# Moving each cycle's products with V behind the first scores two cycles later, in a grouped attention kernel with post-layernorm

## The chip, the cores and the metric

The kernel runs on one core of a Trainium2 chip. The metric is the time of one execution on the device in microseconds (us); lower is better. Weights and inputs are in HBM at the start and the result is in HBM at the end.

## The reference

The layer takes x of 1024 rows by 512 columns in float32. What matters here is the attention:

```python
q = jnp.dot(x, Wq).reshape(b, t, H, HD).transpose(0, 2, 1, 3)        # 32 heads of 16
kv = jnp.dot(x, Wkv).reshape(b, t, G, 2, HD).transpose(2, 3, 0, 1, 4)  # 8 groups, 4 heads each
scores = jnp.einsum('bhqd,bhkd->bhqk', q, k)
scores = jnp.where(causal[None, None], -jnp.inf, scores)
weights = jax.nn.softmax(scores * (1.0 / HD ** 0.5), axis=-1)
ctx = jnp.einsum('bhqk,bhkd->bhqd', weights, v)
```

It is followed by the product with Wo and a bias, a residual and a layernorm, then a feed-forward step (one product with W plus eight low-rank updates), a second residual and a second layernorm.

## The kernel before

**Units and cycles.** The attention is cut into 16 units: a unit `u` is one group of four heads with one half of the queries (512 of them). A unit is worked off in cycles; a cycle is one strip `s` of 256 queries against one pair `p` of key blocks of 128. Units 0 to 7 have 3 cycles each, units 8 to 15 have 7 (8 and up see twice the keys): 80 cycles, numbered 0 to 79. In the profiled execution cycle 0 begins at about 36 us, cycle 24 (the first of unit 8) at 126 us and cycle 79 ends at 302 us.

**What a cycle does.** TensorE computes the scores of a cycle in four pieces (three in a cycle on the diagonal), each one matmul of 512 columns into a PSUM bank of its own (`piece_scores`, L1359). ScalarE takes the exponential of each piece into the SBUF buffer `PB` (L853), GpSimd zeroes the part above the diagonal (L693), and TensorE multiplies the result with V (`accumulate`, L1337), on 32 output columns at a time, into bank 6, which holds both strips of a unit. When a strip is done, ScalarE copies it to SBUF (`evacuate`, L767): after cycles 26, 30, 33, 37, 40 and so on in the second half. The score pieces have three banks that go round, so piece number e waits until the exponential of piece e-3 is done. For unit 15, from cycle 71 on, there are six banks.

**The maxima.** Softmax needs the largest score of each row ahead of the exponentials. TensorE computes scores with the query rows on the partitions ("chunks", L1132, 128 to 512 columns each), VectorE reduces each chunk to its maxima (L907, L914), at the end of a unit L928 joins them, GpSimd splits them into three bfloat16 parts (last step L659, semaphore `nm_parts`), TensorE turns them with four small matmuls (`turn_maxima`, L1141) and ScalarE copies the turned rows (L740), from where a DMA takes them into the queries' tile. The turn for unit u stands at the end of a cycle two or three cycles ahead of the unit (`ROWS_AT`): in the second half at the end of cycles 28, 35, 42, 49, 56, 63 and 70.

**The order.** Each engine's order is written out by hand, cycle by cycle. In a cycle TensorE goes through four places j = 0 to 3. At each it issues a lot of that cycle's chunks (`chunks_of_cycle`, spread by `level`; lot 0 is empty in cycles with three chunks), then score piece j, then a part of a filler. Fillers (`FILL`) are the other work: projections, the transposes and products of finished query blocks. Long fillers (the projections Q, the products `WO` and `FF`, all L1195) have a part at each of the four places, short ones (transposes L1255, L1263, and L1242) at places 1 and 3. ScalarE does in a cycle: the copy of a finished strip, then the exponentials, with a normalisation (`first_norm`, `second_norm`, L785) behind the first of them two cycles after a `WO` or `FF` filler, then copies that belong to fillers and the turned rows. `second_norm` falls into cycles 39, 53 and 67.

**Waits around the products.** The product of a cycle waits for its exponentials and masks; the first one of a strip waits for the copy of the strip before (`raw_out`); ScalarE, with three buffers `PB`, waits ahead of cycle c for the product of cycle c-3 (`pv_done`).

Of the kernel before, what the change touches and what calls it, by code (L numbers as in the profile page):

```python
# [19 lines left out]
def postln_kernel(nc, x, wq, wkv, wo, bo, lora_a, lora_b, w, bias, lora_w, xt, out):  # L20
# [26 lines left out]
    NCYC = len(CYCLES)  # L47
# [19 lines left out]
    def pieces(cyc):  # L67

        first = [(0, range(0, 2), 0), (0, range(2, 4), 0)]
        return first + ([(1, range(0, 4), P)] if on_diagonal(cyc) else [(1, heads, 0) for _, heads, _ in first])  # L70

    def last_of(u, s):
        return CYCLES.index((u, s, 2 * half_of(u) + s))

    LAST_OF = {last_of(u, s): (u, s) for u in range(NU) for s in range(2)}
# [29 lines left out]
    def rows_cycle(u):  # L105

        return (FIRST[u] - (LEAD if u > 3 else 2)) if u else -1
# [39 lines left out]
    for n, job in enumerate(STEPS):  # L147
        b, k = divmod(n, 6)
# [137 lines left out]
    with ctx:  # L286
# [122 lines left out]
        def score_bank(e):  # L409

            return MAX_BANKS + e % ST_BANKS if e < WIDE else (e - WIDE) % (MAX_BANKS + ST_BANKS)
# [296 lines left out]
        def _(act):  # L708
# [22 lines left out]
            def middle_part(n):  # L731

                act.wait_ge(*freed(PROJ[n]))
                nc.scalar.activation(parts[:, n % 2, 1, :], rest[:, n % 2, :], ACT.Copy).then_inc(rest_split, 1)

            def turn_rows(u):
                act.wait_ge(nm_turned, rows_turned(u))
                if u >= 3:
                    act.wait_ge(nm_in, 16 * NPART * (u - 2))
                nc.scalar.activation(NMR[0:NPART * REP, u % 2, :], PS[0:NPART * REP, MISC_BANK["rows", u, 0], :],  # L740
                                     ACT.Copy)\
                    .then_inc(nm_rows, 1)
# [17 lines left out]
            def evacuate(u, s):  # L760
                act.wait_ge(pv_done, last_of(u, s) + 1)
                if u >= G:
                    act.wait_ge(we_split, NC)
                if u >= G + 4:
                    act.wait_ge(wo_split, NC)
                cols = slice(s * HQ, (s + 1) * HQ)
                nc.scalar.activation(RAW[:, u, cols], PS[:, PV_BANK, cols], ACT.Copy).then_inc(raw_out, 1)  # L767
# [19 lines left out]
            def first_norm(b):  # L787
                if b >= 2:
                    act.wait_ge(x1b_ready, b - 1)
                    act.wait_ge(t3_done, b - 1)  # L790
                scaled(X1[b % 2], NORM["WO", b], x1_ready)

            def second_norm(b):
                if b >= 2:
                    act.wait_ge(out_done[b % 2], 16 * (b // 2))
                scaled(OUT[b % 2], NORM["FF", b], out_ready)
# [48 lines left out]
            for cyc in range(NCYC):  # L845
                if cyc >= NP_BUF:
                    act.wait_ge(pv_done, cyc - NP_BUF + 1)
                if cyc - 2 in LAST_OF:
                    evacuate(*LAST_OF[cyc - 2])
                for k in range(len(pieces(cyc))):  # L850
                    e = SCORE_BANKS[cyc] + k
                    act.wait_ge(scores, e + 1)
                    nc.scalar.activation(PB[:, cyc % NP_BUF, k, :], PS[:, score_bank(e), :], ACT.Exp, scale=SCALE)\  # L853
                        .then_inc(probs, 1)
                    if k == 0 and cyc == rows_cycle(1) + 1:
                        turn_rows(1)
                    kind, b, _ = FILL.get(cyc - 2, ("", 0, 0))
                    if k == 0 and kind == "WO":
                        first_norm(b)
                    if k == (0 if cyc < NCYC - 1 else len(pieces(cyc)) - 1) and kind == "FF":  # L860
                        second_norm(b)
                kind, b, _ = job = FILL.get(cyc, ("", 0, 0))
                if job in PROJ or kind in BY_ACT:
                    act_job(JOB[job])
                if FILL.get(cyc - 2, ("",))[0] == "WE":
                    act_job(JOB[FILL[cyc - 2]])
                if FILL.get(cyc - 1) in PROJ:
                    middle_part(PROJ.index(FILL[cyc - 1]))
                if kind == "T2":
                    context_high(b, MISC_BANK[job])  # L870
                if kind == "T3":
                    x1_high(b, MISC_BANK[job])
                if cyc in ROWS_AT and ROWS_AT[cyc] > 1:
                    turn_rows(ROWS_AT[cyc])
                if cyc in WO_HIGH_AT:
                    wo_high_half(WO_HIGH_AT.index(cyc))
# [229 lines left out]
        def _(pe):  # L1106
# [30 lines left out]
            def turn_maxima(u):  # L1137
                was_read(MISC_BEHIND["rows", u, 0])
                pe.wait_ge(nm_parts, u + 1)
                for qb in range(TB):  # L1140
                    last = nc.tensor.matmul(PS[0:NPART * REP, MISC_BANK["rows", u, 0], qb * P:(qb + 1) * P],  # L1141
                                            NMP[:, u % 2, qb, :, :].rearrange("p a j -> p (a j)"),
                                            ident_bf[:, :], start=True, stop=True)
                last.then_inc(nm_turned, 1)
# [179 lines left out]
            def accumulate(cyc):  # L1324

                u, s, p = CYCLES[cyc]
                if on_diagonal(cyc):
                    pe.wait_ge(masked, 3 * sum(1 for c in LAST_OF if c <= cyc))
                pe.wait_ge(probs, SCORE_BANKS[cyc + 1])
                if cyc == 0:  # L1330
                    pe.wait_ge(*freed(FIRST_BEHIND[PV_BANK]))
                if p == 0 and u + s:
                    pe.wait_ge(raw_out, 2 * u + s)
                for k, (i, heads, skip) in enumerate(pieces(cyc)):
                    width = HQ - skip
                    for n, j in enumerate(heads):
                        last = nc.tensor.matmul(PS[32 * j:32 * j + 32, PV_BANK, s * HQ + skip:(s + 1) * HQ],  # L1337
                                                VX[:, key_blocks(cyc)[i], u % G, :],
                                                PB[:, cyc % NP_BUF, k, n * width:(n + 1) * width],
                                                start=(p == 0 and i == 0), stop=(on_diagonal(cyc) and i == 1))  # L1340
                last.then_inc(pv_done, 1)

            def piece_scores(cyc, k):

                u, s, _ = CYCLES[cyc]
                i, heads, skip = pieces(cyc)[k]
                kb = key_blocks(cyc)[i]
                e = SCORE_BANKS[cyc] + k
                if e < ST_BANKS:
                    pe.wait_ge(*freed(FIRST_BEHIND[score_bank(e)]))  # L1350
                elif WIDE <= e < WIDE + MAX_BANKS:
                    pe.wait_ge(max_read, len(CHUNKS))
                elif e >= WIDE + MAX_BANKS + ST_BANKS:
                    pe.wait_ge(probs, e - MAX_BANKS - ST_BANKS + 1)
                elif e >= WIDE:
                    pe.wait_ge(probs, WIDE)
                elif e >= ST_BANKS:
                    pe.wait_ge(probs, e - ST_BANKS + 1)
                nc.tensor.matmul(PS[:, score_bank(e), :], KS[0:NROW, u % G, kb * P:(kb + 1) * P],  # L1359
                                 QS[0:NROW, u % SLOTS, heads[0]:heads[-1] + 1, s * HQ + skip:(s + 1) * HQ],  # L1360
                                 start=True, stop=True).then_inc(scores, 1)

            for cyc, (u, _, _) in enumerate(CYCLES):
                if cyc == 0:
                    rows_moved()
                elif cyc == FIRST[u]:
                    pe.wait_ge(nm_in, 16 * NPART * u)
                for j, lot in enumerate(chunks_of_cycle(cyc)):
                    for n in lot:
                        chunk_scores(n)  # L1370
                    if j < len(pieces(cyc)):
                        piece_scores(cyc, j)
                    if cyc == rows_cycle(1) + 1 and j == 0:
                        turn_maxima(1)
                    filler(cyc, j)
                if cyc:
                    accumulate(cyc - 1)
                if cyc in ROWS_AT and ROWS_AT[cyc] > 1:
                    turn_maxima(ROWS_AT[cyc])
            pe.wait_ge(max_read, len(CHUNKS))  # L1380
            pe.wait_ge(probs, SCORE_BANKS[NCYC - 1])
            pe.wait_ge(*freed(MISC_ORDER[-1]))
# [60 lines left out]
```

## Time and profile before

| | |
|---|---|
| time before, median of 3 runs | 341.67 us (341.11 to 341.87) |
| the profiled execution | 340.83 us, its span 339.1 us |
| TensorE busy | 96% of the span, 2532 matmuls |
| VectorE, ScalarE, GpSimd busy | 76%, 65%, 40% |
| granted TensorE clock | 0.996 of full speed |

The span is the time from the first to the last instruction of the core; the profiled execution is 1.7 us longer than its span. A busy share says how much of the span an engine was working, not that it was at its peak. Matmuls overlap: the next one starts before the last one's recorded end, so that the distance from start to start, and not the recorded duration, is what a matmul costs.

### The profile page before, as it was taken

What the parts mean: (1) busy time and instruction counts of PE and PEld (TensorE: products, weight loads), DVE (VectorE), ACT (ScalarE), POOL (GpSimd) and SP (SyncE); (2) the same over time, 40 slices, a digit from 0 to 9 for tenths busy, and PEclk for the clock granted to TensorE, in tenths of its full rate; (3) what the DMA queues carried; (4) which work ended last, traced back from release to release, by engine and by line L of the source; (5) the groups of instructions that cost most, each with busy time, mean ns of one, the idle gap of its engine ahead of it and who ended that gap; (6) DMA issues with size and microseconds to landing.
All of it is one profiled execution on the core that took longest, in us unless ns stands there. A gap on an engine that the chain in (4) does not pass through costs nothing.

```text
span 339.1 us, 7329 instructions
## 1 busy us (share of the span) xinstructions
PE 324.8 (96%) x2532; PEld 172.2 (51%) x2532; DVE 256.8 (76%) x787; ACT 220.7 (65%) x418; POOL 134.1 (40%) x267
## 2 busy tenths in 40 slices
PE   8999989999999999999999999999999999999993
PEld 3676445455453344454544544544545444458882
DVE  3567978988789889888889789888886961037664
ACT  5754747655767796948757669478585686962431
POOL 8845324443447584347122123211141122321553
PEclk9999999999999999999999999999999999999998
DMA  6886494964145110010010100000000000000002
GB/s 203 297 153 179 119 191 113 252 199 143 37 136 156 45 52 4 3 48 1 3 46 34 50 2 3 0 33 1 3 0 3 34 0 3 2 30 1 2 31 93
DMA packets 15563, 22.96 MB, mean 68 GB/s; under 512 B 1972, under 2 KB 9480, under 8 KB 15528
## 3 DMA queue, kind: packets, MB, share of 16 engines
q1 hardware_dynamic: 15528, 22.51, 24.3%
q8 instruction: 20, 0.33, 0.4%
q14 instruction: 15, 0.12, 0.1%
HBM read 16.29 MB, written 6.03 MB: 66 GB/s over the span
## 4 chain that ended last, share of the span: by engine, by line
PE 74%; DVE 6%; DMA 5%; ACT 5%; issue 4%; SPq 3%; POOL 2%; POOLq 0%; DVEq 0%; ACTq 0%
PE PS L1337 18%; PE PS L1195 17%; PE PS L1132 16%; PE PS L1359 15%; PE PS L1263 2%; ACT PB L853 2%; DMA scr_q<-parts 2%; PE PS L1255 2%; DVE MX L907 2%; DVE scrap L914 2%; DMA X<-in_L_attn_x_turned_dram 1%; DMA QS<-NMR 1%; SPq L489 1%; PE PS L1149 1%; SPq L501 1%
## 5 line engine op out<-in xcount | busy, mean ns | idle before, releaser
L853 ACT ACTIVATE PB<-PS 128x512 f32<-128x512 f32 x288 | 155.2, 601 | 56.5 <-PE PS L1359 55.3
L914 DVE CUSTOM_DVE_ANT_0 scrap<-PS,mask 128x128 bf16<-128x128 f32 (+3 forms) x256 | 111.6, 487 | 18.2 <-PE PS L1132 17.5
L1132 PE MATMUL PS<-KS,QS 96*128 96x512 bf16 (+3 forms) x384 | 107.8, 329 | 2.1 <-DVE MX L907 0.8
L1359 PE MATMUL PS<-QS,KS 99*128 99x512 bf16 x288 | 106.3, 382 | 0.7 <-ACT PB L853 0.6
L907 DVE TENSOR_REDUCE MX<-PS 128x1 f32<-128x512 f32 x128 | 82.0, 684 | 13.2 <-PE PS L1132 12.5
L693 POOL TENSOR_SCALAR_AFFINE_SELECT PB<-PB 128x256 f32<-128x256 f32 (+1 forms) x96 | 46.2, 483 | 106.8 <-ACT PB L853 103.6
L1337 PE MATMUL PS<-PB,VX 128*32 128x256 f32 (+1 forms) x1280 | 78.8, 364 | 0.6 <-ACT PB L853 0.3
L1132 PEld LDWEIGHTS PS<-KS,QS 96*128 96x128 bf16 x384 | 32.8, 97 | 50.4 <-issue 13.7
L1337 PEld LDWEIGHTS PS<-PB,VX 128*32 128x32 f32 x1280 | 33.5, 109 | 42.0 <-issue 19.1
L1195 PE MATMUL PS<-XT,WQ 128*128 128x512 f32 x144 | 45.0, 434 | 1.4 <-ACT NMR L740 0.9
L1359 PEld LDWEIGHTS PS<-QS,KS 99*128 99x128 bf16 x288 | 27.5, 98 | 30.7 <-ACT PB L853 8.4
L1195 PEld LDWEIGHTS PS<-XT,WQ 128*128 128x128 f32 x144 | 26.2, 190 | 10.4 <-ACT NMR L740 2.1
L1195 PE MATMUL PS<-XT 128*128 128x512 f32 x96 | 28.1, 426 | 0.6 <-DVE MX L907 0.6
L1195 PE MATMUL PS<-WQ,XT 128*128 128x512 f32 x96 | 28.2, 426 | 0.0
L674 POOL TENSOR_SCALAR mv<-mv 128x1 f32<-128x1 f32 x15 | 3.4, 227 | 48.6 <-DVE mv L1009 48.5
L914 DVE DVE_READ_ACCUMULATOR2_ANT MX<- 128x1 f32 x256 | 21.3, 83 | 0.0
L1195 PEld LDWEIGHTS PS<-XT 128*128 128x128 f32 x96 | 17.9, 189 | 4.6 <-DVE MX L907 1.1
L1195 PEld LDWEIGHTS PS<-WQ,XT 128*128 128x128 f32 x96 | 17.9, 189 | 4.0
L767 ACT ACTIVATE RAW<-PS 128x256 f32<-128x256 f32 x32 | 12.3, 385 | 11.2 <-PE PS L1337 11.0
L785 ACT ACTIVATE TC<-RAW,shift,rstd 128x512 f32<-128x512 f32 x7 | 5.7, 816 | 13.4 <-POOL shift L676 13.4
L729 ACT ACTIVATE parts<-PS 128x512 bf16<-128x512 f32 x10 | 6.0, 596 | 10.4 <-PE PS L1195 10.4
L684 POOL TENSOR_TENSOR TC<-TC,bias_bc 128x512 f32<-128x512 f32 x8 | 10.3, 1288 | 3.9 <-ACT TC L785 3.9
(92 smaller groups left out, 265.0 us busy)
## 6 DMA issues: line engine op xcount, KB each, us to landing
scr_q<-parts SPq DMA_DIRECT2D x8, 384.0 KB, 3.6
QS<-scr_q SPq DMA_DIRECT2D x15, 192.0 KB, 3.0
X<-in_L_attn_x_turned_dram SPq DMA_DIRECT2D x8, 256.0 KB, 6.3
X<-in_L_attn_x_dram SPq DMA_DIRECT2D x8, 256.0 KB, 3.2
out_dram<-TC SPq DMA_DIRECT2D x8, 256.0 KB, 2.0
QS<-scr_q SPq DMA_DIRECT2D x15, 128.0 KB, 3.1
RAW<-in_L_attn_Wo_dram SPq DMA_DIRECT2D x2, 512.0 KB, 5.8
RAW<-in_L_ffn_W_dram SPq DMA_DIRECT2D x2, 512.0 KB, 8.9
```

The costliest lines, as they stand in the source:

```text
L684: nc.gpsimd.tensor_tensor(X1B[b % 2], X1[b % 2], bias_bc[:, :], ALU.add).then_inc(x1b_ready, 1)
L693: nc.gpsimd.affine_select(out=blk, in_=blk, compare_op=ALU.is_ge, fill=0.0, base=0, pattern=[[0, len(heads)], [1, P]], channel_multiplier=-1)\
L767: nc.scalar.activation(RAW[:, u, cols], PS[:, PV_BANK, cols], ACT.Copy).then_inc(raw_out, 1)
L853: nc.scalar.activation(PB[:, cyc % NP_BUF, k, :], PS[:, score_bank(e), :], ACT.Exp, scale=SCALE)\
L907: nc.vector.tensor_reduce(part[:, j0:j1, 0:1], bank, AX, ALU.max).then_inc(max_read, 1)
L914: last = nc.vector.tensor_tensor_reduce(out=scrap[:, n % 2, (j - j0) * width:(j - j0 + 1) * width], in0=bank[:, j - j0, :], in1=mask[:, HT ...
L1132: last = nc.tensor.matmul(PS[:, CHUNK_BANK[n], k * width:(k + 1) * width], QS[0:ROWS, u % SLOTS, j, qb * P:(qb + 1) * P], KS[0:ROWS, g, k0 ...
L1195: last = nc.tensor.matmul(bank, lhs(a, c), rhs(b, c), start=(k == 0), stop=(k == len(terms) - 1))
L1255: last = nc.tensor.transpose(bank[:, g * P:(g + 1) * P], RAW[:, h * G + g0 + g, qb * P:(qb + 1) * P], ident[:, :])
L1263: last = nc.tensor.transpose(bank[:, c * P:(c + 1) * P], src[:, c * P:(c + 1) * P], ident[:, :])
L1337: last = nc.tensor.matmul(PS[32 * j:32 * j + 32, PV_BANK, s * HQ + skip:(s + 1) * HQ], VX[:, key_blocks(cyc)[i], u % G, :], PB[:, cyc % NP ...
L1359: nc.tensor.matmul(PS[:, score_bank(e), :], KS[0:NROW, u % G, kb * P:(kb + 1) * P], QS[0:NROW, u % SLOTS, heads[0]:heads[-1] + 1, s * HQ + ...
```

## The change

The product of cycle c-1 stood at the end of cycle c, behind the last filler part and ahead of the turn of the maxima. Now the product of cycle c-2 stands in cycle c behind lot 0 of the chunks and the first score piece, and ahead of that place's filler part. In ScalarE's order the copy of a finished strip moves from the start of the cycle to behind the first exponential, ahead of a normalisation that stands there too. No instruction is added or removed.

```diff
             for cyc in range(NCYC):
                 if cyc >= NP_BUF:
                     act.wait_ge(pv_done, cyc - NP_BUF + 1)
-                if cyc - 2 in LAST_OF:
-                    evacuate(*LAST_OF[cyc - 2])
                 for k in range(len(pieces(cyc))):
                     e = SCORE_BANKS[cyc] + k
                     act.wait_ge(scores, e + 1)
                     nc.scalar.activation(PB[:, cyc % NP_BUF, k, :], PS[:, score_bank(e), :], ACT.Exp, scale=SCALE)\
                         .then_inc(probs, 1)
+                    if k == 0 and cyc - 2 in LAST_OF:
+                        evacuate(*LAST_OF[cyc - 2])
                     if k == 0 and cyc == rows_cycle(1) + 1:
                         turn_rows(1)
...
                     if j < len(pieces(cyc)):
                         piece_scores(cyc, j)
+                    if cyc >= 2 and j == 0:
+                        accumulate(cyc - 2)
                     if cyc == rows_cycle(1) + 1 and j == 0:
                         turn_maxima(1)
                     filler(cyc, j)
-                if cyc:
-                    accumulate(cyc - 1)
                 if cyc in ROWS_AT and ROWS_AT[cyc] > 1:
                     turn_maxima(ROWS_AT[cyc])
+            accumulate(NCYC - 2)
```

On TensorE, at the end of cycle 28 and the start of cycle 29, the kernel before has the product of cycle 27 (L1337), then the turn of the maxima (L1141), then the first score piece of cycle 29 (L1359), then a chunk (L1132):

```order
L1132 MATMUL PS<-KS,QS 128x512
L1359 MATMUL PS<-QS,KS 128x512
L1337 MATMUL PS<-PB,VX 32x256 x8
L1141 MATMUL PS<-ident_bf,NMP 12x128 x4
L1359 MATMUL PS<-QS,KS 128x512
L1132 MATMUL PS<-KS,QS 128x128 x4
L1359 MATMUL PS<-QS,KS 128x512
```

The changed kernel has there:

```order
L1132 MATMUL PS<-KS,QS 128x512
L1359 MATMUL PS<-QS,KS 128x512
L1141 MATMUL PS<-ident_bf,NMP 12x128 x4
L1359 MATMUL PS<-QS,KS 128x512
L1337 MATMUL PS<-PB,VX 32x256 x8
L1132 MATMUL PS<-KS,QS 128x128 x4
L1359 MATMUL PS<-QS,KS 128x512
```

The product stood directly ahead of the turn; now a score piece lies between the two, and a score piece stands ahead of each.

On ScalarE, in cycles 36 to 39, the kernel before has eleven exponentials (L853), the copy of the strip finished with cycle 37 (L767), the first exponential of cycle 39, the normalisation (L785), and then the other exponentials:

```order
L740 ACTIVATE NMR<-PS 12x512
L853 ACTIVATE PB<-PS 128x512 x11
L767 ACTIVATE RAW<-PS 128x256
L853 ACTIVATE PB<-PS 128x512
L785 ACTIVATE TC<-TC,shift,rstd 128x512
L853 ACTIVATE PB<-PS 128x512 x10
```

The changed kernel (where the exponential is on line 851) has:

```order
L740 ACTIVATE NMR<-PS 12x512
L851 ACTIVATE PB<-PS 128x512 x12
L767 ACTIVATE RAW<-PS 128x256
L785 ACTIVATE TC<-TC,shift,rstd 128x512
L851 ACTIVATE PB<-PS 128x512 x11
```

The copy and the normalisation now stand side by side between the first and the second exponential of cycle 39.

## Rows read from the trace of the kernel before

**Rows 1.** The page, engines: busy time, share of the span, instructions.
```profile
PE 324.8 (96%) x2532; PEld 172.2 (51%) x2532; DVE 256.8 (76%) x787; ACT 220.7 (65%) x418; POOL 134.1 (40%) x267
...
L853 ACT ACTIVATE PB<-PS 128x512 f32<-128x512 f32 x288 | 155.2, 601 | 56.5 <-PE PS L1359 55.3
...
L1337 PE MATMUL PS<-PB,VX 128*32 128x256 f32 (+1 forms) x1280 | 78.8, 364 | 0.6 <-ACT PB L853 0.3
```

**Rows 2.** Busy time by stretch: us, then PE, PEld, DVE, ACT, POOL, clock, DMA.
```profile
36.00:136.00 100.00, 96.17 (x786) 46.50 (x786) 86.89 (x325) 67.69 (x136) 48.88 (x98) 1.00 0.47 122
136.00:278.00 142.00, 140.38 (x1197) 68.40 (x1199) 121.36 (x340) 102.02 (x195) 40.67 (x91) 1.00 0.05 16
```

**Rows 3.** Timeline, PE, cycles 28 and 29: start us, duration us, engine, line.
```profile
139.34 0.38 PE L1359 MATMUL PS<-QS,KS 99*128 99x512 bf16 x1
139.65 1.07 PE L1337 MATMUL PS<-PB,VX 128*32 128x256 f32 x16
140.53 0.39 PE L1141 MATMUL PS<-ident_bf,NMP 128*12 128x128 bf16 x4
140.85 0.39 PE L1359 MATMUL PS<-QS,KS 99*128 99x512 bf16 x1
```

**Rows 4.** Timeline, PE, cycle 39 and the start of cycle 40.
```profile
174.49 0.86 PE L1337 MATMUL PS<-PB,VX 128*32 128x256 f32 x16
175.28 0.34 PE L1132 MATMUL PS<-KS,QS 96*128 96x384 bf16 x1
175.45 0.38 PE L1359 MATMUL PS<-QS,KS 99*128 99x512 bf16 x1
175.67 0.33 PE L1132 MATMUL PS<-KS,QS 96*128 96x384 bf16 x1
...
176.91 1.07 PE L1337 MATMUL PS<-PB,VX 128*32 128x256 f32 x16
177.91 0.39 PE L1132 MATMUL PS<-KS,QS 96*128 96x512 bf16 x1
```

**Rows 5.** Timeline, ACT, cycle 39.
```profile
175.46 0.38 ACT L767 ACTIVATE RAW<-PS 128x256 f32<-128x256 f32 x1 [0.49 <-PE PS L1337]
175.87 0.60 ACT L853 ACTIVATE PB<-PS 128x512 f32<-128x512 f32 x1
176.36 0.80 ACT L785 ACTIVATE TC<-TC,shift,rstd 128x512 f32<-128x512 f32 x1
177.07 3.18 ACT L853 ACTIVATE PB<-PS 128x512 f32<-128x512 f32 x6
```

**Rows 6.** PE's waits for maxima (us, times, longest); timeline at the turns of units 2, 9.
```profile
PE PS L1195 <- ACT NMR L740: 0.9, 2, 0.7
...
PE PS L1141 <- POOL NMP L659: 0.7, 2, 0.4
...
54.17 0.22 POOL L659 TENSOR_TENSOR NMP<-NM,NMP 128x16 bf16<-128x16 f32 x1
...
54.54 0.38 PE L1141 MATMUL PS<-ident_bf,NMP 128*12 128x128 bf16 x4 [0.24 <-POOL NMP L659]
...
139.25 0.22 POOL L659 TENSOR_TENSOR NMP<-NM,NMP 128x16 bf16<-128x16 f32 x1
```

**Rows 7.** Timeline, DVE and PE, cycle 13.
```profile
88.26 0.29 DVE L914 CUSTOM_DVE_ANT_0 scrap<-PS,mask 128x128 bf16<-128x128 f32 x1 [0.40 <-PE PS L1132]
...
89.34 0.32 PE L1132 MATMUL PS<-KS,QS 96*128 96x384 bf16 x1 [0.24 <-DVE MX L914]
...
90.63 0.34 PE L1132 MATMUL PS<-KS,QS 96*128 96x384 bf16 x1 [0.35 <-DVE MX L914]
```

**Rows 8.** Timeline, ACT and PE, cycle 70, and PE at cycle 75.
```profile
276.91 0.59 ACT L853 ACTIVATE PB<-PS 128x512 f32<-128x512 f32 x1
...
277.55 0.39 PE L1359 MATMUL PS<-QS,KS 99*128 99x512 bf16 x1 [0.29 <-ACT PB L853]
...
291.14 1.07 PE L1337 MATMUL PS<-PB,VX 128*32 128x256 f32 x16 [0.28 <-ACT PB L853]
```

## The prediction

> **What bounds the kernel now.** I read the table of engines first: TensorE is busy 96% of the span, VectorE 76%, ScalarE 65% [rows 1]. The exponentials wait 55.3 us in all for score pieces, and the products with V wait 0.3 us for exponentials [rows 1]: ScalarE waits for TensorE, hardly ever the reverse. Then the busy time by stretch. From 36 to 136 us (units 0 to 7 and the start of unit 8) TensorE is idle for 100.00 - 96.17 = 3.8 us and VectorE is busy for 86.9 of 100 us; from 136 to 278 us TensorE is idle for 142.00 - 140.38 = 1.6 us, and VectorE is busy for 121.4 of 142 us [rows 2]. So in the second stretch nearly every tenth of a microsecond that TensorE takes more goes into the time; in the first, VectorE ends some of TensorE's waits, and part of a cost can be absorbed. Only then did I go to the timelines, since the change adds and removes no instruction: what counts is which neighbours cost more, and which wait loses the product as its cover.
>
> By the end of a cycle's last filler part TensorE has done the same work before and after; only lot 0 and the first score piece come one product earlier. With no waits the burst between two products is just as long, it merely starts at another place. The cost lies in the neighbours, then.
>
> **A. The turn loses its neighbour.** From start to start, a score piece ahead of a product costs 139.65 - 139.34 = 0.31 us; the product, with the turn behind it, 0.88; the turn, with a score piece behind it, 0.32 [rows 3]. A piece among scores costs 0.22 (175.45 to 175.67), and a product with a chunk behind it 177.91 - 176.91 = 1.00 [rows 4]. So entering the products costs 0.31 - 0.22 = 0.09 us, leaving them for scores 1.00 - 0.88 = 0.12, going from product to turn nothing visible. Before: piece, product, turn, piece = 0.31 + 0.88 + 0.32 + 0.22 = 1.73 us. After: piece, turn, piece, product = 0.31 + 0.32 + 0.31 + 1.00 = 1.94, if a piece ahead of the turn costs what it costs ahead of a product. That is +0.21 us a turn; if entering the turn is free, +0.12. I take 0.21: both have few output columns (32 and 12, [rows 3]), and leaving the turn costs 0.32 where the four small matmuls alone, at a quarter of a piece's columns each, would take 0.22. Seven turns (units 9 to 15) stand where TensorE is the bound: 7 x 0.21 = +1.5 us, bounds 0.8 and 1.5.
>
> The Trainium skill, TensorEngine Tiling (Array Packing), Key Properties, says that changing the tiling mode, not just the tile, drains TensorE. It gives no duration; by it each turn apart from the product is one more drain on the way in and one on the way out, which gives the 0.21, and the trace agrees as far as it shows (0.09 in, 0.12 out, nothing between product and turn).
>
> Is the turn's input ready one product earlier? It must be split by GpSimd. At unit 9 the split ends at 139.25 + 0.22 = 139.47; TensorE was ready for the product at 139.65 [rows 3, 6]. At unit 2 the split ends at 54.39 and the turn starts at 54.54, 0.15 later [rows 6], so the unit 9 turn could start at 139.62: no wait, with 0.03 us to spare. Had it to spare nothing in the others, the price is small; I take 0.
>
> **B. The normalisation lands ahead of the piece that TensorE needs.** In cycle 39 ScalarE's row is copy, exponential, normalisation, exponentials. With P the time at which the product of cycle 37 is left (175.28, [rows 4]), the copy starts at P + 0.18 and takes 0.41 to the next start, the normalisation takes 177.07 - 176.36 = 0.71 [rows 5]. After, the order behind P is copy, normalisation, second exponential: the latter starts at P + 0.18 + 0.41 + 0.71 = P + 1.30 and ends at P + 1.90. Its bank is wanted by the first piece of cycle 40, which no longer has the product of cycle 38 ahead of it. A piece starts 277.55 - 276.91 - 0.59 = 0.05 us after the exponential that frees its bank [rows 8], so at P + 1.95. TensorE gets there after three chunks of 384 columns (0.17 each, 175.28 to 175.45), three pieces of 0.22 and the first chunk of cycle 40 at 0.22: P + 1.39. Stall: 0.56 us. Nothing later takes it back. Cycle 53 repeats it. Cycle 67 has two short filler parts of 0.22 more and no first chunk behind it: P + 1.61, stall 0.34. Sum +1.5 us, bounds 0 (if something delays TensorE there anyway) and 1.8.
>
> **C. The copy alone.** In cycles 32, 46 and 60 (chunks of 384 columns, lot 0 of the next cycle empty) the second exponential starts at P + 0.59, frees its bank at P + 1.24, and TensorE is there at 3 x 0.17 + 3 x 0.22 = P + 1.17: 0.07 each, rounded with what smaller bursts add to +0.3. Elsewhere a fourth chunk or the turn gives the time.
>
> **D. Product, then long filler.** The matmul behind a product was a score piece or chunk; in the eight cycles with a `WO` or `FF` filler it is now a float32 matmul with a larger weight load. No row shows that pair. Between 0 and the 0.09 of an entry each: +0.3, bounds 0 and 0.7.
>
> **E. Stalls of the second half that lose their cause.** At 277.55 a piece waits 0.29 us of idle time [rows 8] behind a copy and a context copy on ScalarE; its exponential now starts ahead of the copy. VectorE gets lot 0 of cycle 69 a product earlier, so that a wait of about 0.3 behind it goes too. But the turn of unit 15 then comes before its split is ready and gives most back: net -0.1. In cycles 73 to 76 ScalarE bounds (291.14, [rows 8]) and gets its first piece earlier, and the copy moves behind it: -0.4. The long filler of cycle 65 waits for lot 0's chunk: -0.2. Together -0.7, bounds 0 and -1.2.
>
> **F. The first half.** VectorE sits idle for 0.40 us at 88.26 waiting for lot 0 behind product and turn, and then keeps TensorE waiting at 89.34 and 90.63 (0.24 and 0.35 idle) [rows 7]. With lot 0 ahead of the product it starts about 0.4 earlier, which shortens the stall by as much. Cycles 11, 16 and 22 have a weaker form of it. I take -2.3 for turns 4 to 8 gross, of which their own five switches (5 x 0.21) take 1.1. Turns 2 and 3 are the reverse. They already wait for the split (0.7 in all, [rows 6]) with the product ahead of them; without it they wait 0.9 us longer each, minus the waits of the filler behind the turned rows (0.9 in all), which the product now covers. Exponentials of the cycle before, with the first piece done early, end some 0.3 earlier and the split with them: +0.2 each. With 0.1 for unit 1, the half comes to -2.3 + 1.1 + 0.4 + 0.1 = -0.7; bounds -3.8 (all of TensorE's idle time there) and +2.0 (no gain, the turns' 1.1 and 0.4 doubled).
>
> **Sum.** +1.5 + 1.5 + 0.3 + 0.3 - 0.7 - 0.7 = +2.2 us. The profiled execution took 340.83 us, its span of 339.1 and 1.7 around it, so it would take 343.0; the median of the runs before is 341.67, 0.84 above it, and the forecast on it is **343.9 us**.
>
> **The rivals.**
> *VectorE is fed better (faster).* Lot 0 ahead of the product gives VectorE work during it, everywhere. If F brings 3.8 and E 1.2, they outweigh the 0.8 to 1.5 of A as soon as B stays under 2 us; with A at 0.8, B and C at 0.5 and D 0: -3.0 + 0.6 = about -2.4, 339.3 us. For it: the idle 0.40 [rows 7]. Against: in the second stretch there is only 1.6 us of idle time to win [rows 2]. It decides from F at -3.
> *Nothing measurable.* The rotation is neutral as the count of work says, B and C do not show because TensorE is late at cycle 40 anyway, held up by a chunk whose bank VectorE has not read, and the first half pays for most of A: 1.5 + 0.3 (A, D) - 0.7 - 0.9 (E, and F a little better) = +0.2, 341.9 us.
> *The turns stay exposed (much slower).* If DMA rows, splits and turned rows slip with the turn, each of the seven turns of the first half waits the 0.9 us of a product, and the stalls of VectorE remain: +2.2 + 0.7 + 7 x 0.4 = +5.7, 347.4 us. Against: at unit 9 the input was ready [rows 6].
>
> **How the numbers follow.** Forecast 0.54, faster rival 0.17, no change 0.18, much slower 0.11. What this kernel's measurement can tell from no change is about 0.2%, 0.7 us: below 341.0 is faster, above 342.4 slower. The forecast has a little in "no change" (0.03), the no-change rival a little on either side. Faster 0.17, same 0.20, slower 0.63. The forecast's own range, with the bounds of B and F, is 342.2 to 345.6; the common range leaves out most of the faster rival and of the much slower one: 340.9 to 345.8.
>
> **What the profile after would show.** A: at each turn of the second half 0.31 us from piece to turn, 0.32 to the next piece, and 1.00 from the product on. B: a wait of TensorE's score pieces for exponentials of 0.5 us at the starts of cycles 40 and 54, with L767 and L785 side by side; the total of that wait rises from 0.6 us to over 1.5. F: VectorE without the gap behind the turns of units 4 to 8, and fewer waits of chunks between 81 and 123 us. The prediction is wrong if the score pieces' wait stays at 0.6 us, or if the start of cycle 24 comes earlier by 2 us or more.

## The result and the profile after

| | before | changed |
|---|---|---|
| median of 6 runs each | 341.67 us | 343.91 us |
| lowest and highest | 340.98, 342.12 | 342.96, 345.28 |
| ratio to before | | 1.0071, 95% interval 1.0047 to 1.0094 |
| the profiled execution, its span | 340.83, 339.1 us | 344.25, 342.5 us |

The changed kernel is slower by 0.7%, between 1.6 and 3.2 us. The forecast was 343.9 us.

The page of the changed kernel, engines and the two groups that answer to [rows 1]:

```profile
PE 327.4 (96%) x2532; PEld 171.0 (50%) x2532; DVE 256.5 (75%) x787; ACT 222.5 (65%) x418; POOL 134.0 (39%) x267
...
L851 ACT ACTIVATE PB<-PS 128x512 f32<-128x512 f32 x288 | 160.2, 601 | 67.7 <-PE PS L1359 64.5
...
L1337 PE MATMUL PS<-PB,VX 128*32 128x256 f32 (+1 forms) x1280 | 78.8, 364 | 0.1
```

The shares are nearly the same, and so is the work. The idle time before the products fell from 0.6 us [rows 1] to 0.1. It is the waits of others that grew. The changed kernel's list of PE's waits, which answers to [rows 6]: who waited for whom, us in total, times, longest:

```profile
PE PS L1141 <- POOL NMP L659: 2.4, 4, 0.9
...
PE PS L1359 <- DMA QS<-NMR: 0.8, 1, 0.8
...
PE PS L1359 <- ACT PB L851: 0.4, 2, 0.2
```

The turn's wait for its split went from 0.7 us [rows 6] to 2.4, and a score piece now waits 0.8 us for a DMA; it did not show in the list before.

These totals do not tell where the time went: idle time is counted from a matmul's recorded end, and that end lies behind the next one's start (in [rows 4], 175.45 + 0.38 = 175.83 against 175.67). A better measure is at hand. At the start of the second score piece of a cycle both kernels have issued exactly the same work, so the difference of the two start times is what the order has cost up to there. The differences of the two profiled executions, read from the timelines (all cycles where it steps by over 0.05 us from the cycle before):

```
cycle      0     3     5     8     9    10    11    12    13    14    16    17    19    20    22    23
sum    +0.29 +1.08 +1.50 +2.00 +2.19 +2.41 +2.32 +2.15 +2.37 +2.06 +2.29 +1.70 +2.03 +1.90 +2.04 +1.66
step   +0.29 +0.79 +0.42 +0.49 +0.19 +0.22 -0.09 -0.17 +0.22 -0.31 +0.22 -0.58 +0.33 -0.12 +0.13 -0.38

cycle     25    26    29    30    31    33    36    37    40    43    44    45    47    50    51    54
sum    +1.54 +1.46 +1.69 +1.55 +1.65 +1.76 +1.95 +2.04 +2.43 +2.65 +2.52 +2.62 +2.73 +2.93 +3.01 +3.40
step   -0.12 -0.07 +0.22 -0.13 +0.10 +0.09 +0.23 +0.08 +0.39 +0.22 -0.13 +0.10 +0.09 +0.24 +0.09 +0.39

cycle     57    58    59    61    64    65    68    70    71    72    75    76    79
sum    +3.62 +3.50 +3.59 +3.71 +3.90 +3.52 +3.66 +3.30 +3.74 +3.84 +3.79 +3.44 +3.40
step   +0.22 -0.13 +0.10 +0.09 +0.24 -0.38 +0.13 -0.36 +0.43 +0.11 -0.06 -0.35 -0.04
```

The last sum, 3.40 us, is the difference of the spans (342.5 - 339.1). Of it 0.29 lies before cycle 0, where nothing was changed. The rest, 3.11, lies at the upper end of what the timed runs allow.

**The turn (A).** The changed kernel's PE timeline at the end of cycle 28 and in cycle 29, which answers to [rows 3]: start us, duration us.

```profile
140.80 0.38 PE L1359 MATMUL PS<-QS,KS 99*128 99x512 bf16 x1
141.11 0.39 PE L1141 MATMUL PS<-ident_bf,NMP 128*12 128x128 bf16 x4
141.43 0.39 PE L1359 MATMUL PS<-QS,KS 99*128 99x512 bf16 x1
141.75 1.07 PE L1337 MATMUL PS<-PB,VX 128*32 128x256 f32 x16
142.76 0.40 PE L1132 MATMUL PS<-KS,QS 96*128 96x128 bf16 x4
```

From start to start: 0.31 from piece to turn, 0.32 on to the piece, 0.32 into the product, 1.01 out of it. The forecast had 0.31, 0.32, 0.31, 1.00. Entering the turn from a piece costs what entering the products costs, 0.31 for a piece that takes 0.22 elsewhere.

Of what the rows name, the turn (bfloat16, 12 columns) and the products (float32, 32 columns) share against the pieces and chunks the few output columns and the 128 rows. The rows and the type do not explain the price: the short filler of cycle 29, float32 with 128 rows where pieces have 99, starts 0.22 us behind its piece (142.99 to 143.21) and is left for a chunk after 0.22 (to 143.43), which is no surplus, and the same kind of filler ahead of a product takes 0.31 (142.75 to 143.06 in the kernel before).

**The copy and the normalisation (B).** PE and ACT in cycles 39 and 40, which answer to [rows 4, 5]. PE:

```profile
177.70 0.34 PE L1132 MATMUL PS<-KS,QS 96*128 96x384 bf16 x1
...
178.86 0.38 PE L1132 MATMUL PS<-KS,QS 96*128 96x512 bf16 x1
179.46 0.39 PE L1359 MATMUL PS<-QS,KS 99*128 99x512 bf16 x1 [0.22 <-ACT PB L851]
179.78 1.07 PE L1337 MATMUL PS<-PB,VX 128*32 128x256 f32 x16
```

ACT:

```profile
177.83 0.38 ACT L767 ACTIVATE RAW<-PS 128x256 f32<-128x256 f32 x1 [0.16 <-PE PS L1337]
178.12 0.80 ACT L785 ACTIVATE TC<-TC,shift,rstd 128x512 f32<-128x512 f32 x1
178.82 2.05 ACT L851 ACTIVATE PB<-PS 128x512 f32<-128x512 f32 x4
```

With P = 177.70 the copy starts at P + 0.13 and the normalisation at P + 0.42; the second exponential starts at P + 1.12, and the piece that needs its bank at P + 1.76. Without the wait it would have started 0.22 behind the chunk at 178.86, at 179.08: a stall of 0.38 us where 0.56 was forecast. The copy starts 0.05 us sooner behind the product and takes 0.29 to the next start where the row before showed 0.41, so the exponential is 0.18 earlier than I had it. The 0.41 was not the price of the copy: the exponential behind it had to wait for its piece, which ends at 175.45 + 0.38 = 175.83 [rows 4] and was followed at 175.87 [rows 5].

### The profile page after: what moved, and what is told of

Read it like the earlier page. It is cut to its first block, busy times and chain, and to the rows that moved or that the text cites. A ratio compares the mean times of both kernels' runs of the same rounds, so it can differ in the third digit from the quotient of the medians.

```text
span 342.5 us, 7337 instructions
## 1 busy us (share of the span) xinstructions
PE 327.4 (96%) x2532; PEld 171.0 (50%) x2532; DVE 256.5 (75%) x787; ACT 222.5 (65%) x418; POOL 134.0 (39%) x267
## 4 chain that ended last, share of the span: by engine, by line
PE 76%; DMA 5%; DVE 5%; ACT 3%; issue 3%; SPq 3%; POOL 3%; POOLq 0%; DVEq 0%
PE PS L1337 19%; PE PS L1195 18%; PE PS L1132 16%; PE PS L1359 16%; PE PS L1263 2%; DMA scr_q<-parts 2%; PE PS L1255 2%; DVE scrap L914 2%; DMA X<-in_L_attn_x_turned_dram 1%; PE PS L1141 1%; ACT PB L851 1%; DVE MX L907 1%; DMA QS<-NMR 1%; SPq L489 1%; PE PS L1149 1%
## 5 line engine op out<-in xcount | busy, mean ns | idle before, releaser
L851 ACT ACTIVATE PB<-PS 128x512 f32<-128x512 f32 x288 | 160.2, 601 | 67.7 <-PE PS L1359 64.5
L1132 PE MATMUL PS<-KS,QS 96*128 96x512 bf16 (+3 forms) x384 | 105.9, 329 | 1.9 <-DVE MX L907 0.8
L1359 PE MATMUL PS<-QS,KS 99*128 99x512 bf16 x288 | 106.4, 381 | 1.2 <-DMA QS<-NMR 0.8
L1337 PE MATMUL PS<-PB,VX 128*32 128x256 f32 (+1 forms) x1280 | 78.8, 364 | 0.1
L1132 PEld LDWEIGHTS PS<-KS,QS 96*128 96x128 bf16 x384 | 32.2, 97 | 55.4 <-issue 21.0
L1337 PEld LDWEIGHTS PS<-PB,VX 128*32 128x32 f32 x1280 | 33.5, 109 | 40.7 <-issue 14.8
L1359 PEld LDWEIGHTS PS<-QS,KS 99*128 99x128 bf16 x288 | 27.6, 98 | 26.3 <-ACT PB L851 7.1
L767 ACT ACTIVATE RAW<-PS 128x256 f32<-128x256 f32 x32 | 12.4, 388 | 4.6 <-PE PS L1337 4.4
L785 ACT ACTIVATE TC<-RAW,shift,rstd 128x512 f32<-128x512 f32 x7 | 5.7, 817 | 13.4 <-POOL shift L676 13.4
L580 POOL TENSOR_TENSOR parts<-TC,parts 128x512 bf16<-128x512 f32 x8 | 9.3, 1160 | 6.2 <-DVE NMP L937 3.3
```

What stands on the lines that cost most here:

```text
L580: nc.gpsimd.tensor_tensor(parts[:, s, 2, :], rest[:, s, :], parts[:, s, 1, :], ALU.subtract)\
L1132: last = nc.tensor.matmul(PS[:, CHUNK_BANK[n], k * width:(k + 1) * width], QS[0:ROWS, u % SLOTS, j, qb * P:(qb + 1) * P], KS[0:ROWS, g, k0 ...
```

## The experiments

Each is compared with the kernel before on the same chip, whose median was 341.52 us beside the first four runs and 341.42 beside the others. Steps are read as in the table above. From cycle 10 on they agree between executions of the same order to 0.02 us, so one profile tells more of a step than the timed runs tell of the whole. Ahead of it a wait for a DMA can shift what follows: the step at cycle 5 is 0.41 to 0.43 in five profiles with this order on TensorE and 0.53 in a sixth.

**The changed kernel again.**

> The changed kernel itself, once more, to tell what belongs to it from what belongs to one execution. Theory: the steps against the kernel before are the same again within 0.05 us at every cycle from 3 on, the 0.79 us before cycle 3 among them; only the offset of 0.29 us that is there before cycle 0 differs. Rival (the small steps are scatter between executions): they turn up at other cycles.

345.01 us in one run. The offset before cycle 0 is 0.82 us, the step at cycle 3 is 1.19 and there is none at cycle 9 (0.01); from cycle 10 on every step is that of the first execution within 0.01 us. So the start and the steps at cycles 3 and 9 scatter, and there the expected 0.05 us was missed; the others belong to the order. A wait at cycle 3 is there in both, of unequal length.

**The turn moved away from the product in the kernel before.**

```diff
-                if cyc in ROWS_AT and ROWS_AT[cyc] > 1:
+                if cyc in ROWS_AT and 1 < ROWS_AT[cyc] < 4:
                     turn_maxima(ROWS_AT[cyc])
...
                     if j < len(pieces(cyc)):
                         piece_scores(cyc, j)
...
+                    if j == 0 and ROWS_AT.get(cyc - 1, 0) > 3:
+                        turn_maxima(ROWS_AT[cyc - 1])
```

> The kernel before, with every product in its old place and only the turn of the maxima of units 4 to 15 moved behind the first score piece of the next cycle, so that a piece lies between product and turn. Theory A (neighbours cost): a step of 0.21 to 0.24 us appears against the kernel before at the turns of units 9 to 14, 1.3 us together, although no product moved. Rival (the 0.22 us steps belong to the product's new place, for instance to what ScalarE and VectorE get later): no step at the turns here. If ScalarE's copy of the turned rows between first and second exponential holds up the next cycle's first piece, a further step of up to 0.3 us shows one cycle later.

345.17 us in one run, the last sum 3.81 without the 0.42 before cycle 0. The steps at cycles 29, 36, 43, 50, 57, 64 and 71 are 0.22, 0.22, 0.22, 0.22, 0.22, 0.22 and 0.21 us. Together with 0.44 at cycles 30, 44 and 58 that is 2.85 us; the rest lies ahead of cycle 25, where units 4 to 8 turn later too. No product moved here. Theory A holds, and its rival falls. The 0.44 is larger than the 0.3 expected; it is the short filler of cycles 29, 43 and 57, whose bank is the one with the turned rows. PE and ACT of this kernel in cycle 29:

```profile
141.07 1.07 PE L1339 MATMUL PS<-PB,VX 128*32 128x256 f32 x16
142.08 0.39 PE L1361 MATMUL PS<-QS,KS 99*128 99x512 bf16 x1
142.40 0.39 PE L1143 MATMUL PS<-ident_bf,NMP 128*12 128x128 bf16 x4
142.72 0.40 PE L1134 MATMUL PS<-KS,QS 96*128 96x128 bf16 x4
...
143.68 0.44 PE L1265 MATMUL PS<-ident,TC 128*128 128x128 f32 x2 [0.35 <-ACT NMR L740]
```

```profile
143.06 0.57 ACT L740 ACTIVATE NMR<-PS 12x512 bf16<-12x512 f32 x1
```

The product is left after 142.08 - 141.07 = 1.01 us, the piece is left for the turn after 0.32 and the turn after 0.32: one entry and one exit more than before.

The Trainium skill, TensorEngine Tiling (Array Packing), Key Properties, says that a change of the tiling mode drains TensorE. This run fits it, if the turn's 12 columns count as a mode other than the pieces': 0.22 us appears for one pair of changes more. Whether they do, and which part of the 0.22 is a drain, no row tells.

**The turn joined to the product again, in the changed kernel** (the same two edits on the changed order, so that the turn stands right behind the product).

> The changed kernel, with the turn of the maxima of units 4 to 15 issued right behind the product that now stands behind the first score piece of the next cycle, so that product and turn are neighbours again (ScalarE copies the turned rows behind the first exponential of that cycle). Theory A (entering and leaving the products and the turn costs 0.09 and 0.12 us, and the change pays both once more per turn): each of the steps of 0.22 to 0.24 us at the turns of units 9 to 14 vanishes, 1.3 us there, and about as much again at units 4 to 8 and 15 where the turn also gets a product more of time for its split: the time falls by 1.5 to 2.5 us against the changed kernel, to 341.4 to 342.4. Rival (the turn of each unit costs 0.2 us because its input, split by GpSimd, is just ready, not for its neighbours): the steps of units 9 to 14, whose inputs are ready, do not change; only units 4 to 8 and 15 gain, together under 1 us.

Median 345.40 us of 4 runs, ratio 1.0107 (1.0085 to 1.013). That is 1.5 us above the changed kernel by the medians, 1.2 by the ratios, whose intervals just overlap; the last sum without the start is 3.94 against 3.11. A fall of 1.5 to 2.5 us was expected, and it did not come. The part for which the run was made did come out: the steps at cycles 29, 36, 43, 50, 57 and 64 are all 0.00 instead of 0.22 to 0.24, and unit 15's pair (cycles 70 and 71) is -0.75 in place of +0.07. What I had not counted is that the turned rows come one product later for those who wait for them. Its PE waits:

```profile
PE PS L1134 <- ACT NMR L740: 2.4, 3, 1.3
...
PE PS L1134 <- DMA QS<-NMR: 0.9, 1, 0.9
```

Steps of +0.32 (cycle 11), +0.77 (17), +0.53 (19) and +1.07 (24) stand where the changed kernel has -0.09, -0.58, +0.33 and 0.00, and at cycles 30, 44 and 58 the filler in the turned rows' bank waits (+0.22 where it was -0.13). The price of the neighbours is right; what the delay of the turned rows costs was missing from the expectation.

**The normalisation ahead of the copy.**

```diff
                     if k == 0 and kind == "WO":
                         first_norm(b)
                     if k == (0 if cyc < NCYC - 1 else len(pieces(cyc)) - 1) and kind == "FF":
                         second_norm(b)
+                    if k == 0 and cyc - 2 in LAST_OF:
+                        evacuate(*LAST_OF[cyc - 2])
```

> The changed kernel, with ScalarE's copy of a finished strip behind the normalisation instead of ahead of it (cycles 39, 53, 67, 74). Theory B (the second exponential is late because copy and normalisation both stand behind the end of the product): the normalisation now runs during the product, the second exponential starts about 0.5 us after the product is left, and the step of 0.39 us that TensorE's trace shows between cycles 39 and 40 and again between 53 and 54, and the 0.13 us before cycle 68, fall to under 0.1: the time falls by 0.8 to 0.9 us against the changed kernel, to about 343.1. Rival (the first piece of cycle 40 is late for a chunk's bank that VectorE has not read): the steps stay at 0.39 and the time at 343.9.

Median 344.64 us of 4 runs, ratio 1.009 (1.0057 to 1.0122), which does not differ from the changed kernel within the intervals. The steps at cycles 40 and 54 fell from 0.39 to 0.12 and the one at 68 from 0.13 to -0.02, together 0.69 us. That is theory B's direction and most of its size: 0.12 remains where under 0.1 was expected, because the second exponential starts 0.85 us behind the end of the product and not 0.5 (180.07 to 180.92 in the profile). The forecast of the time, 343.1, was missed: cycle 75 has +0.63 instead of -0.06. PE there:

```profile
294.99 1.07 PE L1337 MATMUL PS<-PB,VX 128*32 128x256 f32 x16 [0.81 <-ACT RAW L767]
```

In cycle 74 ScalarE works without a gap (291.81 to 297.29), the copy of unit 14's last strip now stands behind 0.83 us of normalisation, and unit 15's first product waits for that copy. The mend is right for `second_norm` and wrong for cycle 74. The profiled execution has 2.81 us before cycle 0, where nothing was edited; with such starts four runs say little of 0.1 us in the order. Without that offset its last sum is 2.92, against 3.11 of the changed kernel.

**The copy in its old place, the products in the new.**

```diff
+                if cyc - 2 in LAST_OF:
+                    evacuate(*LAST_OF[cyc - 2])
                 for k in range(len(pieces(cyc))):
...
-                    if k == 0 and cyc - 2 in LAST_OF:
-                        evacuate(*LAST_OF[cyc - 2])
```

> The changed order on TensorE, but ScalarE copies a finished strip at the start of the cycle as before, so ahead of the first exponential. Theory B (ScalarE's queue behind the end of the product sets the first piece of the next cycle): the first exponential now waits for the product too, the second is about 0.5 us later than in the changed kernel, and steps of 0.5 us each appear in every cycle with a finished strip and no turn or filler behind it (32, 46, 60) and 0.4 us more at cycles 39 and 53: the time rises by 2 to 4 us against the changed kernel. Rival (ScalarE has slack): no change.

346.93 us in one run, 3.0 us above the changed kernel's median, its span 2.7 us above the changed kernel's. The steps at cycles 33, 47 and 61 are 0.45, 0.48 and 0.45 instead of 0.09, those at 40 and 54 are 0.93 instead of 0.39, that at 68 is 0.67 instead of 0.13. TensorE's wait for exponentials ahead of score pieces is 2.2 us in all, 0.4 in the changed kernel. So what stands in ScalarE's queue behind the product can set the first piece of the next cycle. The change's second edit is needed: without it the first would cost 2.6 to 2.9 us more (the last sum here is 5.98 with -0.01 before cycle 0, against 3.40 with 0.29).

**Old places for the products of cycles 0 and 1.**

```diff
-                    if cyc >= 2 and j == 0:
+                    if cyc >= 2 and j == 0 and cyc - 2 >= 2:
                         accumulate(cyc - 2)
...
+                if cyc and not (cyc - 1 >= 2):
+                    accumulate(cyc - 1)
```

The copy of cycle 0's strip stands in its old place too, ahead of the exponentials of cycle 2.

> The products of cycles 0 and 1 stand where they stood in the kernel before; from the product of cycle 2 on the order is that of the changed kernel. Theory (the first piece of cycle 3 waits for the DMA that brings unit 1's turned rows, which lands at the same moment in both traces, 49.5 us; before, the product of cycle 1 filled that wait): the step of 0.79 us before cycle 3 vanishes and the time falls by about 0.8 us against the changed kernel, to 343.1. Rival (the wait is one execution's late DMA and no property of the order): no change, 343.9, and the changed kernel run again shows no such wait.

Median 343.49 us of 10 runs, ratio 1.0057 (1.004 to 1.0074). The step at cycle 3 is -0.14, where the four profiles with the product behind the first piece of cycle 3 and the copy behind the first exponential have +0.40 to +1.19; the other three profiles with the old order up to cycle 3 have -0.06 to -0.11. The wait for the DMA is gone from the list. One profile stands apart: the run above with the copy in its old place has the products in the new one, and +0.34 at cycle 2 with +0.05 at cycle 3 in place of the wait. Its time is 0.4 us under that of the changed kernel where 0.8 was expected, and the intervals don't separate the two; the trace does. The cause can be read in three rows. PE before:

```profile
48.36 1.07 PE L1337 MATMUL PS<-PB,VX 128*32 128x256 f32 x16
49.50 0.39 PE L1359 MATMUL PS<-QS,KS 99*128 99x512 bf16 x1
```

PE changed:

```profile
49.48 0.39 PE L1359 MATMUL PS<-QS,KS 99*128 99x512 bf16 x1 [0.76 <-DMA QS<-NMR]
```

The first piece of cycle 3 follows the last of the three DMA issues of unit 1's turned rows by 3.9 us in both (45.56 to 49.50, 45.62 to 49.48), and by 3.5 to 4.0 us in the three other profiles that wait there. Before, the product of cycle 1 (1.00 us to leave) was done while the rows were on their way; now TensorE waits and does the product afterwards.

**The new order from cycle 11 on** (the products of cycles 0 to 8 in their old places, with `>= 9` for `>= 2` above, and the copies of those strips in their old place).

> The products of cycles 0 to 8 stay in their old place, those from cycle 9 on have the new one. Theory (the steps of the two traces add up: +0.79 at cycle 3, +0.42 and +0.49 at the turns of units 2 and 3 and +0.22 at that of unit 4 go, the -0.74 us between cycles 11 and 23 stays, the +1.74 of the second half stays): 1.0 us above the kernel before, 342.6 and about 1.3 us below the changed kernel. Rival (the gain of cycles 11 to 23 only gives back what the cycles ahead of them lost): the gain goes with the loss, and the time is 1.7 us or more above the kernel before.

Median 343.05 us of 10 runs, ratio 1.0041 (1.0023 to 1.0059): 1.6 us above the kernel before by the medians, 0.8 to 2.0 by the interval, which holds the expected 1.0 and the rival's 1.7. The timed runs do not decide; the steps do. The steps of cycles 10 to 23 that belong to the new order are there (-0.16, +0.22, -0.31, +0.22, -0.58, +0.33, -0.12, +0.12, -0.36 from cycle 12 on), with none at cycles 3, 5, 8 and 10, so the gain does not depend on the loss ahead of it. In the profiled execution a wait of 1.19 us for a DMA stands at cycle 9, in a stretch whose order is that of the kernel before; the next run, with the same order there, has 0.00. Without it the last sum is +1.02, as expected. How often that wait occurs is not known, and the timed runs would carry it.

**The parts that pay, together.** Besides the order from cycle 11 on: the turns of units 10, 12, 14 and 15 behind the product, and the normalisation ahead of the copy only where it is a `second_norm`. ScalarE copies the rows of these four turns behind the first exponential of the next cycle.

```diff
+                    if j == 0 and ROWS_AT.get(cyc - 1) in (10, 12, 14, 15):
+                        turn_maxima(ROWS_AT[cyc - 1])
...
+                    if k == 0 and cyc - 2 in LAST_OF and kind == "FF":
+                        evacuate(*LAST_OF[cyc - 2])
```

> As the run from cycle 11 on, and besides: in cycles 39, 53 and 67 the normalisation stands ahead of the copy; the turns of units 10, 12, 14 and 15 stand right behind the product of the next cycle. Theory (the steps add up: +1.0, less 0.27 + 0.27 + 0.15 for the normalisation, less 3 x 0.24 for three turns and 0.8 at unit 15): 1.2 us under the kernel before, about 340.3 us. Rival (each mend moves the wait to the next queue): no better than the kernel before, 341.5 or more.

Median 340.04 us of 12 runs, ratio 0.9962 (0.9944 to 0.998): faster than the kernel before by 1.3 us (0.7 to 1.9), as expected, and by the two ratios some 3.7 us faster than the changed one. The last sum is -0.77 with +0.44 before cycle 0, -1.21 for the order. The steps added up: cycle 36, 50 and 64 have 0.00, cycles 40 and 54 have 0.12, cycles 68 and 71 have +0.01 and -0.39. Cycle 39 of this kernel on ACT:

```profile
175.38 0.80 ACT L785 ACTIVATE TC<-TC,shift,rstd 128x512 f32<-128x512 f32 x1
176.09 0.37 ACT L767 ACTIVATE RAW<-PS 128x256 f32<-128x256 f32 x1
176.35 2.06 ACT L853 ACTIVATE PB<-PS 128x512 f32<-128x512 f32 x4
```

The product of cycle 37 is left at 175.51 here: the normalisation runs while it is under way, and the second exponential starts at P + 0.84 instead of P + 1.12.

## Why the prediction was right

The forecast of +2.2 us met a measured difference of the medians of 2.24. Term by term, by the steps of the table:

| | forecast | measured |
|---|---|---|
| A, turns of units 9 to 15 | +1.5 | +1.4 for six, about +0.2 for unit 15 |
| B, normalisation in cycles 39, 53, 67 | +1.5 | +0.9 (0.39, 0.39, 0.13) |
| C, copy alone | +0.3 | +0.3 (three of 0.09), but not by the copy |
| D, product ahead of a long filler | +0.3 | +0.6 in six cycles (0.10, 0.08, 0.10, 0.09, 0.10, 0.11); two more lie inside E |
| E, stalls of the second half | -0.7 | -1.6 |
| F, units 0 to 7 | -0.7 | +1.4 |

The measured column sums to 3.2 with rounding; the trace has 3.11 from cycle 0 to the end, the timed runs 2.24. Part of the distance is the wait at cycles 3 and 9, 0.98 us in this execution, which scatters. The direction was right, and so were the mechanisms of A, B and D and the named parts of E. That the sum was right to 0.1 us is luck: B and E were too high, D and F were too low, and C had the right size from a wrong cause.

The prediction also named signs by which to call it wrong. One came true by the letter: the score pieces' wait for exponentials was to rise from 0.6 us to over 1.5, and the list has 0.4. The sign was badly chosen. The list counts from the recorded end of the chunk ahead, so that the stall of 0.38 us at cycle 40 stands there as 0.22; the 0.4 is this one and its like at cycle 54, and the two waits that made up the 0.6, one of them that of 277.55 [rows 8], are gone. The steps and the two experiments on ScalarE's order show B where the list does not. The other sign did not come: the second piece of cycle 24 starts 1.66 us later than before, and not 2 us or more earlier.

- **A** is shown, by the changed kernel's rows (steps of 0.22 to 0.24 us), by the turn moved alone in the kernel before (0.21 to 0.22 each), and by the turn joined again, which takes the steps of units 9 to 14 to 0.00.
- **B**: the step is the one named, at the cycles named; the size was 0.39 for 0.56, because the copy takes 0.29 to the next start and not 0.41. For cycle 67, 0.13 came for 0.34. Moving the normalisation removes 0.69 us of it.
- **C** came in size, 0.09 for 0.07 each, and not in cause. Cycle 32 of the changed kernel, PE and ACT:

```profile
154.38 0.38 PE L1359 MATMUL PS<-QS,KS 99*128 99x512 bf16 x1
...
155.15 0.69 PE L1359 MATMUL PS<-QS,KS 99*128 99x512 bf16 x2
```

```profile
154.34 0.38 ACT L767 ACTIVATE RAW<-PS 128x256 f32<-128x256 f32 x1 [0.16 <-PE PS L1337]
154.80 2.06 ACT L851 ACTIVATE PB<-PS 128x512 f32<-128x512 f32 x4
```

  The copy would let ScalarE go on at 154.34 + 0.29 = 154.63. The second exponential starts at 154.80, behind its piece, which ends at 154.38 + 0.38 = 154.76. So the piece is late, because it now stands behind the product, and the copy fits into the wait. The forecast's 0.41 [rows 5] held a wait of the same kind. This is read from rows; no run took the copy away in these cycles.
- **D**, the pair that no row showed, costs 0.11 us in each of the eight cycles, a little above the bound of 0.09, and not at the exit: TensorE leaves the product after 1.00 us as elsewhere. The filler's first three matmuls then take 149.27 - 148.47 = 0.80 us in cycle 31, where before the piece and these three took 147.62 - 146.71 = 0.91, so 0.69 without the piece's 0.22. In cycles 65 and 77 the 0.11 lies inside larger steps, so D is 0.9 in all and E is -1.8. Why the filler takes longer there was not tried.
- **E** was mis-sized. Its named parts came: -0.38 at cycle 65 for -0.2, -0.45 from cycle 75 to 77 for -0.4; at unit 15 -0.36 and +0.43, a turn's 0.2 in it, net about -0.1. On top came -0.13 at each of cycles 30, 44 and 58 and -0.04 at 35, 49 and 63, -0.19 at 25 and 26, which I had not named. Before, the short filler of cycle 29 starts 0.07 us late and its second matmul 0.05; in the changed kernel it does not. The rows of the kernel before point to the copy of the turned rows, whose bank this filler takes: it runs from 140.96 to 141.55, and the filler starts at 141.60. In the changed kernel the turn is one product earlier. The moved turn, with its 0.35 us wait of this filler for the copy, fits.
- **F** failed: the forecast was -0.7 us, the steps sum to +1.4. The mechanism that was to give the gain was there. In cycle 13 VectorE goes from L928 straight to the chunk, where it had waited 0.40 us [rows 7]:

```profile
89.83 0.19 DVE L928 TENSOR_REDUCE NM<-MX 128x16 f32<-128x32 f32 x1
89.95 0.29 DVE L914 CUSTOM_DVE_ANT_0 scrap<-PS,mask 128x128 bf16<-128x128 f32 x1
```

  Cycles 14, 17 and 23 win back 0.31, 0.58 and 0.38. From cycle 10 to 23 the order gains 0.53 us in sum, turns included, where -1.2 was forecast. Two steps were wrong besides. Turns 2 and 3 cost 0.42 and 0.49, not 0.2: the split does not come 0.3 us earlier. At unit 2 its last step stands at 55.14 where it stood at 54.17, 0.97 later, while TensorE was 1.08 behind from cycle 3 on, and the turn again starts 0.15 behind the split's end. The rows fit that the second piece, which now stands behind the product, sets the exponentials and masks that GpSimd does first; no run tried it. And the wait for the DMA with unit 1's rows, +0.79, was not in the sum at all, which gave unit 1 0.1 us. It could have been seen: the product of cycle 1 took 1.14 us from start to start where the others take 1.00.

Of the rivals, the faster one was right that VectorE is fed better; that was worth most in the first half (cycles 14, 17 and 23) and 0.38 us at cycle 65 of the second, not enough to outweigh A and B; the no-change rival fell with the steps at cycles 40 and 54, where the piece waits for an exponential and not a chunk. The much slower one had the right mechanism for turns 2 and 3 and, with 0.13 to 0.33 at turns 4 to 8, not for the rest. The faster rival's sum of "-3.0 + 0.6" does not follow from its terms: 0.8 and 0.5 make +1.3 against -3.8 and -1.2, so -3.7 us.

## What to carry to other kernels

When a change only moves work on the bound engine, price its new and old neighbours from start to start: here 0.21 us per turn followed from four rows. Then list everything that the moved block had been covering, DMAs still on their way included, and look at the block's own duration for signs of a covered wait. Do not take a total of waits as the sign of a stall, since here it fell from 0.6 to 0.4 us while two stalls of 0.39 appeared. Because the steps of two traces at points of equal work repeat to 0.02 us away from waits for DMAs, a change that loses as a whole can be cut at the places where it pays: here the same order, without the early cycles and with four turns and three copies placed otherwise, is 1.3 us faster than the kernel before.

## What the runs showed of the hardware

The products' matmuls have 32 output columns and the turn's have 12. With the turn directly behind it a product is left after 0.88 us, with a matmul of 128 columns behind it after 1.00. Setting the two apart by a piece of 128 columns costs 0.21 to 0.22 us (seven times in one run), and joining them again takes it back (0.00 at six turns in another). Which of the 0.22 belongs to which change is an attribution: only the pair is measured.

A float32 filler with 128 columns takes 0.11 us longer for its first three matmuls behind a product than behind a bfloat16 piece (0.80 against 0.69, cycle 31). The time before cycle 0 differed by up to 2.8 us between profiled executions of kernels that are the same up to there.
